# Layer 1's shared-key attention: 48-row maxima for two heads at a time, all units of a step after the third score

## The reference

```python
q = (x @ Wq)          # (2048, 16 heads, 16)
k, v = x @ Wk, x @ Wv # (2048, 16), one for all heads
s = q . k / sqrt(16), positions after the query masked
y = softmax(s) @ v, heads joined, @ Wo + bo
x = layernorm(x + y)
```

## Time and profile before

| | |
|---|---|
| median of 3 runs | 1902.28 us (1901.07 to 1902.51) |
| the profiled execution | 1903.28 us |
| its span, first to last instruction | 1901.5 us |
| TensorE matmul busy | 1662.2 us (87%) |
| VectorE busy | 1018.7 us (54%) |
| ScalarE busy | 765.5 us (40%) |
| GpSimd busy | 410.2 us (22%) |
| mean granted TensorE clock | 0.941 of full |

### The profile page before, as it was taken

How to read it: one execution, slowest core, us unless ns; L and a number is a source line. 1 busy time by engine, 2 the same in 40 slices (tenths; PEclk the granted TensorE clock), 3 DMA queues, 4 the chain that set the end, 5 groups by cost and what they waited for, 6 DMA issues and landing times.

```text
span 1901.5 us, 25145 instructions
## 1 busy us (share of the span) xinstructions
PE 1662.2 (87%) x9820; PEld 989.9 (52%) x9820; DVE 1018.7 (54%) x1695; ACT 765.5 (40%) x1779; POOL 410.2 (22%) x458
## 2 busy tenths in 40 slices
PE   7985688889999999699988658986999999978998
PEld 4664343333333335345564425664777777763556
DVE  4666665577787762432226683325567666732222
ACT  3421245557767776211101211115666666641111
POOL 3222301000000000400000018713444444420000
PEclk9997788899999999799999879987999999998999
DMA  4000310000000002000001120000000000010000
GB/s 152 2 2 15 100 40 1 2 1 1 1 1 1 1 2 93 0 0 1 0 14 45 52 61 0 1 1 5 7 1 7 1 7 1 1 67 25 11 11 23
DMA packets 28501, 36.12 MB, mean 19 GB/s; under 512 B 5472, under 2 KB 24608, under 8 KB 27872
## 3 DMA queue, kind: packets, MB, share of 16 engines
q1 hardware_dynamic: 28384, 34.52, 5.7%
HBM read 24.91 MB, written 2.10 MB: 14 GB/s over the span
## 4 chain that ended last, share of the span: by engine, by line
PE 66%; DVE 15%; issue 7%; POOL 7%; ACT 3%; DMA 1%; SPq 1%; POOLq 0%; DVEq 0%; ACTq 0%
PE PS L966 6%; PE PS L1244 6%; PE PS L953 6%; PE PS L1250 6%; PE PS L928 5%; PE PS L1263 5%; PE PS L2030 3%; PE PS L2019 2%; PE PS L1997 2%; PE PS L1669 2%; POOL arena L2215 2%; PE PS L330 2%; PE PS L1650 2%; PE PS L1003 2%; PE PS L1972 2%
## 5 line engine op out<-in xcount | busy, mean ns | idle before, releaser
L1190 DVE TENSOR_REDUCE arena<-PS 128x1 f32<-128x1024 f32 (+7 forms) x320 | 330.1, 1061 | 129.2 <-PE PS L930 92.9
L1076 ACT ACTIVATE arena<-PS 128x512 f32<-128x512 f32 (+3 forms) x640 | 318.0, 533 | 162.1 <-PE PS L953 71.5
L953 PE MATMUL PS<-arena 99*128 99x512 bf16 (+3 forms) x640 | 207.5, 355 | 1.9 <-ACT arena L1076 1.3
L928 PE MATMUL PS<-arena 96*128 96x512 bf16 (+3 forms) x640 | 181.9, 363 | 24.6 <-DVE arena L1190 21.7
L190 POOL TENSOR_TENSOR rstd<-ve,mhalf 128x4 f32<-128x4 f32 x32 | 32.3, 1011 | 611.3 <-DVE ve L216 611.3
L966 PE MATMUL PS<-arena 128*32 128x512 f32 (+3 forms) x1280 | 153.4, 552 | 2.8 <-ACT arena L1082 1.7
L185 ACT ACTIVATE XT<-PS 128x1024 f32<-128x1024 f32 x32 | 32.8, 1024 | 291.5 <-PE PS L178 291.5
L953 PEld LDWEIGHTS PS<-arena 99*128 99x128 bf16 x640 | 60.8, 100 | 152.2 <-ACT arena L1076 115.2
L1244 PE MATMUL PS<-XT,arena 128*128 128x512 f32 x256 | 122.7, 602 | 15.1 <-DVE arena L2412 10.6
L1294 DVE TENSOR_TENSOR arena<-arena,PS 128x512 f32<-128x512 f32 x64 | 44.0, 688 | 164.0 <-PE PS L1250 163.9
L1279 ACT ACTIVATE arena<-PS 128x512 f32<-128x512 f32 x64 | 38.2, 597 | 232.7 <-PE PS L1244 232.7
(11 more groups left out here) (234 smaller groups left out, 2849.1 us busy)
## 6 DMA issues: line engine op xcount, KB each, us to landing
arena<-arena SPq DMA_DIRECT2D x55, 128.0 KB, 2.4
XT<-in_L_attn_xT SPq DMA_DIRECT2D x4, 512.0 KB, 7.7
X<-in_L_attn_x SPq DMA_DIRECT2D x4, 512.0 KB, 9.3
arena<-in_L_attn_out_w SPq DMA_DIRECT2D x1, 2048.0 KB, 7.7
out<-X SPq DMA_DIRECT2D x4, 512.0 KB, 2.9
arena<-in_dmask SPq DMA_DIRECT2D x1, 1024.0 KB, 5.6
arena<-in_L_ffn_W_up SPq DMA_DIRECT2D x1, 1024.0 KB, 4.8
arena<-in_L_ffn_W_gate SPq DMA_DIRECT2D x1, 1024.0 KB, 6.9
```

Of the source, the lines that this page charges most:

```text
L928: last = pe.matmul(flat[:, o:o + w], q, a.KS[0:SROWS, CH * kc:CH * kc + w], start=True, stop=kc < c)
L953: last = pe.matmul(PS[:, b, lo:CH], a.KS[0:rows, P * j:P * (j + 1)], a.QS[0:rows, G1 * g + r, CH * c + lo:CH * (c + 1)], start=True, stop= ...
L1076: act.activation(a.PB[:, n % 3, r, lo:CH], PS[:, 4 + x % 3, lo:CH], ACT.Exp, scale=D0 ** -0.5).then_inc(a.e2, 1)
L1190: dve.tensor_reduce(dst, src, AX.X, ALU.max, negate=True).then_inc(a.m1, 1)
```

## The change

Maxima are made from three products of parts (high with high, high with middle, middle with high: 48 rows, `PACK`) instead of six. The rows of `QS` are reordered so that the first 48 are these; the scores still use all 96. A copy of the first 48 rows for the odd heads (`QO`) and for the keys (`KO`) goes to partitions 64 to 111, by one DMA each a chunk. A unit is now a pair of heads with up to 512 keys: one matmul from partitions 0 to 47, one from 64 to 111, into two banks. There are 320 units as before, with the same number in each step and the same columns to reduce. From chunk 1 on the partial maxima are joined by a small reduction. All units of a step stand between score 2 and score 3, and the values after score 3. The parts' buffers move: chunk 0's and 3's to places of their own in the arena, chunk 1's and 2's into columns of `QS` that are not yet stacked; `AN` of chunk 0 lies on chunk 3's parts, the rest on finished columns of `QS`. So the first exponential waits for chunk 0's stacks alone, and the first `normed` still for all. SP stacks in halves, in a new order. Layer 1's feed-forward part gets its raw weights at other addresses. The masks of `krow` and the repetition of `Wk` follow the new row order.

```diff
+PACK = 3 * D0
+ODD = 64
+HALF_DMAS = 6
...
-                        self.units += [(i, t, h, 1, 0, 2, CH), (i, t, h, 1, 2, 2, n),
-                                       (i, t, h + 1, 1, 0, 2, CH), (i, t, h + 1, 1, 2, 2, n)]
+                for pair in range(G1 // 2):
+                    for kc in range(c + 1):
+                        self.units.append((i, t, pair, kc, P * (t + 1) if kc == c else CH))
...
+    def first_rows(c):
+        if c >= 2:
+            sp.wait_ge(a.second_half, 16 * HALF_DMAS * c)
+        if c == 3:
+            sp.wait_ge(a.low, 2 * c + 2)
         sp.wait_ge(a.ev, 2 * c + 1)
+        stack(c, a.hb, 0, a.first_half)
+        stack(c, a.hb, 2, a.first_half)
         sp.wait_ge(a.mid, c + 1)
+        stack(c, a.mb, 1, a.first_half)
+        sp.wait_ge(a.first_half, 16 * HALF_DMAS * (c + 1))
+        if c >= 1:
+            sp.wait_ge(a.odd, 16 * 2 * c)
+        cols = slice(CH * c, CH * (c + 1))
+        sp.dma_start(a.QO[ODD:ODD + PACK, :, cols], a.QS[0:PACK, 1:H:2, cols]).then_inc(a.odd, 16)
+        sp.wait_ge(a.low, 2 * c + 2)
+        sp.dma_start(a.KO[ODD:ODD + PACK, cols], a.KS[0:PACK, cols]).then_inc(a.odd, 16)
+
+    def other_rows(c):
+        if c >= 1:
+            sp.wait_ge(a.second_half, 16 * HALF_DMAS * c)
+        stack(c, a.hb, PACK + 2, a.second_half)
+        stack(c, a.mb, PACK + 1, a.second_half)
+        stack(c, a.lb, PACK, a.second_half)
...
+    first_rows(0)
+    other_rows(0)
+    first_rows(1)
     maxima_rows(0)
-    stack_chunk(3)
+    other_rows(1)
+    maxima_rows(1)
+    first_rows(2)
+    other_rows(2)
+    maxima_rows(2)
+    first_rows(3)
+    other_rows(3)
...
-        for e in range(nh):
-            q = a.QS[0:SROWS, G1 * g + h0 + e, CH * c + P * t:CH * c + P * (t + 1)]
...
+        pe.matmul(PS[:, b, 0:n], a.QS[0:PACK, h, at], a.KS[0:PACK, keys], start=True, stop=kc < c)
+        last = pe.matmul(PS[:, b + 1, 0:n], a.QO[ODD:ODD + PACK, h // 2, at], a.KO[ODD:ODD + PACK, keys], start=True, stop=kc < c)
+        if kc == c:
+            for e in range(2):
+                last = pe.matmul(PS[:, b + e, n - P:n], k.identb[:, :], a.mqb, start=False, stop=True)
...
         if scored:
-            score(n + 1, 0)
-        for u in units[:half]:
+            for r in range(G1 - 1):
+                score(n + 1, r)
+        for u in units:
             unit(u)
         if scored:
-            score(n + 1, 1)
+            score(n + 1, G1 - 1)
         if 0 <= n < P1.nb:
             value(n)
-        if scored:
-            score(n + 1, 2)
-        for u in units[half:]:
-            unit(u)
-        if scored:
-            score(n + 1, 3)
...
         if n == 0:
-            for par in range(2):
-                act.wait_ge(a.stack[par], 16 * SPLIT_DMAS * 2)
+            act.wait_ge(a.first_half, 16 * HALF_DMAS)
+            act.wait_ge(a.second_half, 16 * HALF_DMAS)
...
         if i == 0:
-            for par in range(2):
-                pool.wait_ge(a.stack[par], 16 * SPLIT_DMAS * 2)
+            pool.wait_ge(a.first_half, 16 * HALF_DMAS * NC)
+            pool.wait_ge(a.second_half, 16 * HALF_DMAS * NC)
...
+        dst = a.NM[:, i % 2, t, heads] if c == 0 else a.MA[:, i % 2, kc, t, heads]
+        dve.tensor_reduce(dst, PS[:, b:b + 2, 0:n], AX.X, ALU.max, negate=True).then_inc(a.m1, 1)
```

More of the change, by code:

```diff
@@ L107, in constants @@
     c["denrow"] = (i[:, None] == 32 * np.arange(4)[None, :] + D0).astype(f)
[L108 to L109 removed]
+    first, p = i < PACK, np.where(i < SROWS, i % 3, -1)
+    high, mid = np.where(first, (p == 0) | (p == 1), p == 0), np.where(first, p == 2, p == 1)
+    c["krow"] = np.stack([high, (i >= SROWS) & (i < SROWS + MROWS), mid, ~first & (p == 2)], 1).astype(f)
     inv = (1.0 / 10000.0 ** (np.arange(0, 64, 2, dtype=f) / f(64))).astype(f)
@@ L675 @@
 QKV1 = QK1 + D0
-SPLIT_DMAS = 12
+PACK = 3 * D0
+ODD = 64
+HALF_DMAS = 6
 G1 = 4
@@ L785, in l1_alloc @@
     a.KS = take([P, T], BF16)
+    a.QO = take([P, H // 2, T], BF16)
+    a.KO = take([P, T], BF16)
     a.VX = take([P, NT, 32])
-    a.AN = take([P, H // 4, T])
+    first_parts = o
     a.PB = take([P, 3, 4, CH])
-    parts_at = o - 21 * CH
-    a.hb, a.mb, a.lb = (v(parts_at + 6 * CH * i, [P, NC, 3, CH], BF16) for i in range(3))
-    a.r1 = v(parts_at + 18 * CH, [P, 3, CH])
     a.OT = take([P, 2, CH])
@@ L811, in l1_alloc @@
     assert o <= 41000, o
+    last_parts = o
+    words = v(0, [P, H, T // 2])
+    first = v(o, [P, H // 4, 2, CH // 2])
+    later = [words[:, H // 2:H, CH // 2 * c:CH // 2 * (c + 1)].rearrange("p (g u) n -> p g u n", u=2) for c in range(NC - 1)]
+    a.AN = [first] + later
+    in_arena = lambda at: [v(at + 3 * CH // 2 * i, [P, 3, CH], BF16) for i in range(3)]
+    in_stack = lambda c: [a.QS[:, 3 * i:3 * i + 3, CH * c:CH * (c + 1)] for i in range(3)]
+    a.hb, a.mb, a.lb = zip(in_arena(first_parts), in_stack(2), in_stack(3), in_arena(last_parts))
+    a.r1 = words[:, 9:15, CH // 2 * 3:CH // 2 * 4]
     s = k.sem
@@ L867, in l1_sp @@
         sp.dma_start(a.wo[32 * r:32 * r + D0, :, :], wo[r]).then_inc(a.ldo, 16)
-    for i in range(1, NI1):
+    for i in range(3, NI1):
         maxima_rows(i)
@@ L913, in unit @@
     def unit(u):
-        i, t, h0, nh, kc0, nkc, n = P1.units[u]
+        i, t, pair, kc, n = P1.units[u]
         c, g = i // 4, i % 4
@@ L917, in unit @@
         if u == 0 or P1.units[u - 1][0] // 4 != c:
-            pe.wait_ge(a.stack[c % 2], 16 * SPLIT_DMAS * (c // 2 + 1))
-            pe.wait_ge(a.low, 2 * c + 2)
+            pe.wait_ge(a.first_half, 16 * HALF_DMAS * (c + 1))
+            pe.wait_ge(a.odd, 16 * 2 * (c + 1))
         if x >= 2:
             pe.wait_ge(a.m1, x - 1)
-        for e in range(nh):
-            q = a.QS[0:SROWS, G1 * g + h0 + e, CH * c + P * t:CH * c + P * (t + 1)]
[L924 to L930, removed]
+        b = 2 * (x % 2)
+        h = G1 * g + 2 * pair
+        at = slice(CH * c + P * t, CH * c + P * (t + 1))
+        keys = slice(CH * kc, CH * kc + n)
+        pe.matmul(PS[:, b, 0:n], a.QS[0:PACK, h, at], a.KS[0:PACK, keys], start=True, stop=kc < c)
[3 more added lines that the diff above has]
+                last = pe.matmul(PS[:, b + e, n - P:n], k.identb[:, :], a.mqb, start=False, stop=True)
         last.then_inc(a.s1, 1)
@@ L1002, in out @@
         for g in range(4):
-            last = pe.matmul(f_tile(k, j, F1_BANK), a.AN[:, g, P * t:P * (t + 1)], a.wo[:, g, :], start=g == 0, stop=g == 3)
+            last = pe.matmul(f_tile(k, j, F1_BANK), a.AN[c][:, g, j // 2, P * (j % 2):P * (j % 2 + 1)], a.wo[:, g, :], start=g == 0, stop=g == 3)
         if j == TPC - 1:
@@ L1208, in l1_dve @@
             unit(u)
-            if u in P1.last_unit and P1.units[u][0] >= 8:
+            if u in P1.last_unit and P1.units[u][0] >= 4:
                 combine(P1.units[u][0])
```

94 lines of the change are left out of this document (35 added, 59 removed).

## The result

| | before | after |
|---|---|---|
| median | 1901.67 us (4 runs, 1900.17 to 1902.51) | 1932.43 us (4 runs, 1928.49 to 1934.29) |
| the profiled execution, its span | 1903.28, 1901.5 us | 1928.49, 1926.7 us |
| mean granted TensorE clock | 0.941 | 0.927 |

The ratio is 1.016 with a 95% interval of 1.0142 to 1.0178: slower by 1.6%, where 1900 us had been forecast.

A forecast was written before the change was run, and what follows sets the result against it. TensorE was taken to bind by a hair over VectorE, with steps of 2.65 to 2.70 us. Terms -7.5 - 3.9 - 4.2 + 7.0 + 5.3 + 1.0 = -2.4 gave a median of 1899.9, said as 1900; range 1887 to 1913.

The forecast's parts named there:

- Pairs stream together: Layer 1's maxima matmuls: two heads' 48-row matmuls stream at once, saving half the columns, 2.9, 4.6, 6.4 us a group.
- a change of division: TensorE switching between whole array and halves or column strips: 0.10 us each, +0.20 per step for entering and leaving units.
- the third score after the turned inverse sums: Once a group, the third score waits for ScalarE's copy with only two scores between: +0.40 us.
- The slower rival: VectorE's round bounds two-unit steps, not TensorE: steps of 2.8, +11 us, 1911; chance 0.20, late stacks counted with it.
- any other of the rivals: Faster, division changes hide: 1891 us, chance 0.22; pairs apart (1945 to 1955) or half's weights not loaded ahead (1917): 0.05.
- Blocks 92 to 138: Chunk 3's two-unit steps: -2.8 us a group, 2.7 groups in blocks 96 to 138, -7.5 us.
- The first exponential: At the start, it no longer waits for the last stack and could come at about 257.3: -2.3 us.
- chunk 1: Two-unit steps there: -1.2 us in each of three groups, -0.6 for the 1.2 GHz clock after stalls; -4.2 us.
- Three or four units in a step: The third unit waits for the first one's drain, fourth score and values queued behind: mean 0.44 over 16 three-unit steps, +7.0 us.
- The four steps with four units: In chunk 0, lying in its stalls or at 1.2 GHz before and after: counted as 0.
- The start: GpSimd's first product waits for all stacks, 287.2 rather than 286.09, group 3's maxima queued behind: +1.0 us, bounds -2.3 to +10.
- Steps without units: Blocks 139 on: fourth score waits for the first one's bank; +0.43 in nine, +0.28 in three, +0.13 in five: +5.3 us.

The follow-up runs named there:

- the other profile: The changed kernel, but steps without units have their values after the second score; the same kernel up to block 138: 1925.59 us, ratio 1.0118.
- all three edits: Changed kernel with third and fourth units after the values, values after the second score in steps without units, first two groups' normed results on own words: 1898.75 us.

## Why the prediction was wrong

Right were the steps at the full clock with two units. Pairs stream together; a change of division is 0.10; full steps are 2.61 to 2.74 (2.65 to 2.70 forecast), and the third score after the turned inverse sums is 0.41 late (0.40 forecast). The slower rival, VectorE's round, is not what happened: its reductions are as short as before; nor is any other of the rivals. Blocks 92 to 138 came to -5.5, 2.0 short, since the narrow steps gain nothing (steps 94 to 96 together +0.2). The first exponential came earlier than forecast, at 255.1; the first score itself was 2.6 earlier, in the run with one matmul of zeros only 0.1, so that this is not the edit's alone. That chunk 1 came near its forecast (-3.6 for -4.2) is partly luck: in the runs with one matmul of zeros, with the third unit moved and with the normed results moved, the same steps gave -1.1, with more half clock behind GpSimd's stalls.

Some figures of the working were off and changed little. The terms as written add up to -2.3, not -2.4. The 32-row f32 matmuls of the earlier trace rows would take 0.215 each one after another, not 0.11 (their four sets start 0.22 apart, and one f32 matmul of 512 columns takes 0.86 in the run with zeros): 3.4 us rather than 1.7 against 1.15, which speaks for "together" even more.

Two steps of the forecast failed, and a third was sized too small.

*Three or four units in a step: "4.3 ... mean 0.44: +7.0".* The mechanism was right, and the full-width step is 4.05. But the mean was not taken from each step's own row: in the kernel with one matmul of zeros, steps 35 to 42 lose 0.66, 1.19, 1.82, 0.81, 0.52, 0.11, 0.34 and 0.31, 5.8 in all, where about 3.5 was forecast; 38 and 39 had been 2.90 and 2.82, and around GpSimd's stall (36, 37) nothing takes the wait up (some of step 37's is clock, 0.54 for 0.65). Then the term had no price for the granted clock. The text said of chunk 1 that "after its stalls the clock is at 1.2 GHz", and used it only as a gain; that the new waits of 1.1 in every step would, with 48-row units, keep the clock down behind such a stall was in no term and no rival. In steps 37 to 41 it was 0.50 throughout: the values of 512 columns take 1.94 rather than 1.07, and the steps 4.7 to 6.5. They are 6.5 us longer than with the zeros (27.95 less 21.42), most of the 8.4. "The four steps with four units ... I count 0" was wrong too: these are steps 7 to 10, and one after the other they lost 0.8, 5.5 (step 8, with the late product), 1.1 and 0.2. Unforeseen as well were steps 1 and 2, of two units each: +2.8, at clocks of 0.50 and 0.82 where they had been at 1.00. Steps 0 to 7 lost 4.4 together, and 1.3 with the order of before. The misses are 12.2 in blocks 35 to 47, 2.7 in 80 to 91 and 3.1 (4.4 - 1.3) in steps 0 to 7: 18 of the 27 us between the forecast's -2.4 and the +24.5 measured at block 159.

*The start: "+1.0".* The range given, -2.3 to +10, held what was measured (+7.9), but the value was at its near end, and the +11.9 of the other profile lies outside. SP issued two of the three last sets of six stacks in 5.4 and 5.7, not 3.9; chunk 3's first stacks were issued by 280.4 (276.54 + 3.84) and the odd heads' copy only at 284.4, a stand of 4.0 where the estimate had a landing of 2.4. So the product was 7.3 later than before (293.37 for 286.09), and group 3's maxima behind it too: step 8 alone is +5.5.

*Steps without units: "+0.43 in nine"* was 0.58 in six full steps with a projection, and "+0.13 in five" was 0.82 in steps 150 and 155: +6.8 for +5.3. The mechanism was right and the size too small. Part of it is a sum: 0.47 + 0.60 + 0.05 is 1.12, not 1.08, and 1.13 was measured.

## What to carry to other kernels

Price a new wait on TensorE twice, once for its own length and once for what the granted clock takes afterwards: here 1.1 us of waiting in each of eight steps cost 7.3 us where one matmul of zeros filled most of the waits, and 8.4 us more where TensorE stood idle in them and the clock stayed at half behind a stall. Don't carry the clock's price from one kernel to another: the waits with 96-row units left it at 0.91, the 48-row units without the waits at 0.90, and both together at 0.72. Take the cost of a new floor from each step's own row, not from a mean over steps that differ. And where an instruction moves behind a chain of DMA issues, look at what is queued behind it on its own engine, and put the longest stand of the queue into the estimate.

## What the runs showed of the hardware

- Two bf16 matmuls of 48 rows, in rows 0 to 47 and 64 to 111, start within 0.01 us and stream 512 columns in 0.22 together; in the same rows they start 0.22 apart.
- An f32 matmul of 512 columns into 15 columns of the array takes 0.86 alone (start to start, in the run with four of them); the four values' matmuls with 32 columns each take 0.9 together (635.44 to 636.44, less a change of division).
- The cost of the half clock does not add up over edits: it was 37 us of blocks 35 to 47 in the changed kernel, 21 with the normed results moved, 17 with the third unit moved, 7 with all three edits (0.72, 0.83, 0.84 and 0.93 of 66.0, 60.4, 53.4 and 50.4 us). The same kernel repeats it (37 us again in a second profile, whose blocks came 4 us later). What makes it 21 with the normed results moved, where units, order and waits are the same, was not found, which sets a limit to how well such a kernel can be forecast.
- TensorE's granted clock behind a stall of 3 us: where 48-row units and waits of 1.1 us in each step came together, it stayed at 0.50 for the next five steps (28 us, in two profiles); with either one alone these steps were granted 0.85, and a third kernel with both got 0.72.
